# A graph layer on one core: mixer and gate groups of two tiles laid between expert tiles, norms in place, sums in freed columns

## What is computed

```python
xn = layernorm(x)
agg = segment_sum(xn[src] * edge_weight[:, None], dst)           # 106250 gathered rows
x2 = x + agg @ gnn_weight + mix(xn)                              # mix: linear attention over all rows
y = layernorm(x2)
top, idx = top_k(y @ gate_w + gate_b, 2); w = softmax(top)        # 16 experts, two for each row
moe = sum_k w[k] * (relu(y @ w1[idx[k]] + b1[idx[k]]) @ w2[idx[k]] + b2[idx[k]])
out = x2 + layernorm(y + moe) * gamma + beta
```

## Time and profile before

| | us |
|---|---|
| median of 3 runs | 1696.25 |
| lowest, highest | 1687.12, 1700.92 |
| the profiled execution | 1693.13 |
| its span (first to last instruction) | 1691.4 |
| outside the span | 1.7 |

### The profile page before, as it was taken

How to read it: one execution, slowest core, us unless ns; L and a number is a source line. 1 busy time by engine, 2 the same in 40 slices (tenths; PEclk the granted TensorE clock), 3 DMA queues, 4 the chain that set the end, 5 groups by cost and what they waited for, 6 DMA issues and landing times. The chain is left out here.

```text
span 1691.4 us, 25276 instructions
## 1 busy us (share of the span) xinstructions
PE 1204.5 (71%) x7570; PEld 944.3 (56%) x7570; DVE 586.8 (35%) x1778; ACT 490.3 (29%) x1323; POOL 1005.6 (59%) x1090
## 2 busy tenths in 40 slices
PE   0299989887605899885589887898968764356670
PEld 0155545556503788673378776777757653345560
DVE  6345445444500322332032231233213344344334
ACT  4033334332201333331133232233323232122221
POOL 3577777776377777677777767767763133231203
PEclk9999999999756999998699989898989887588885
DMA  9486333334245689787568968868994575545762
GB/s 336 138 277 205 106 104 106 105 104 117 63 163 184 181 275 321 239 293 239 193 183 308 324 241 315 305 223 301 398 309 162 212 270 168 202 149 206 256 240 84
DMA packets 173617, 363.98 MB, mean 215 GB/s; under 512 B 27968, under 2 KB 109248, under 8 KB 173344
## 3 DMA queue, kind: packets, MB, share of 16 engines
q1 hardware_dynamic: 80896, 186.89, 30.7%
q0 software_dynamic: 49296, 134.68, 25.6%
q10 hardware_dynamic: 43280, 40.65, 7.2%
HBM read 302.20 MB, written 59.90 MB: 214 GB/s over the span
## 5 line engine op out<-in xcount | busy, mean ns | idle before, releaser
L625 POOL DMA_INDIRECT ring<-normed_rows,src_sb x831 | 797.6, 960 | 331.9 <-issue 288.4
L1252 PE MATMUL ps<-room 128*128 128x128 f32 x2368 | 330.8, 300 | 56.2 <-DMA room<-in_w1b 42.3
L1252 PEld LDWEIGHTS ps<-room 128*128 128x128 f32 x2368 | 313.6, 214 | 66.5 <-issue 54.0
L1265 PE MATMUL ps<-room 128*128 128x256 f32 x1184 | 294.9, 394 | 16.3 <-issue 10.6
L1063 DVE TENSOR_TENSOR aggT<-ps,room 128x256 f32<-128x256 f32 x173 | 73.1, 423 | 612.4 <-PE ps L1265 572.7
L616 POOL DMA_INDIRECT ring<-results_by_slot,slot_i x98 | 97.5, 995 | 266.9 <-DMA results_by_slot<-aggT 125.4
L1265 PEld LDWEIGHTS ps<-room 128*128 128x128 f32 x1184 | 224.7, 200 | 45.1 <-issue 19.1
L739 ACT ACTIVATE room<-ps,room 128x128 f32<-128x128 f32 x592 | 168.8, 368 | 217.4 <-PE ps L1252 213.5
L1128 PE MATMUL ps<-ring,S 128*32 128x256 f32 x1680 | 119.9, 424 | 133.1 <-issue 102.2
L1155 PE MATMUL ps<-room,tT 128*128 128x512 f32 x392 | 181.6, 607 | 0.1
L1128 PEld LDWEIGHTS ps<-ring,S 128*32 128x32 f32 x1680 | 53.6, 118 | 170.9 <-issue 132.8
(11 more groups left out here) (148 smaller groups left out, 1143.8 us busy)
## 6 DMA issues: line engine op xcount, KB each, us to landing
room<-in_w2b SPq DMA_DIRECT2D x119, 640.0 KB, 5.7
room<-in_w1b SPq DMA_DIRECT2D x119, 514.0 KB, 6.4
room<-rows_by_slot SPq DMA_DIRECT2D x173, 128.0 KB
results_by_slot<-aggT ACTq DMA_DIRECT2D x173, 128.0 KB
ring<-normed_rows,src_sb POOLq DMA_INDIRECT x831
normed_rows<-X SPq DMA_DIRECT2D x7, 896.0 KB, 8.1
X<-in_x ACTq DMA_DIRECT2D x49, 128.0 KB, 2.4
result<-ring SPq DMA_DIRECT2D x49, 128.0 KB, 1.9
```

Of the source, the lines that this page charges most:

```text
L625: pool.indirect_dma_start(out=ring[:, b % 2 * BT + m, :], out_offset=None, in_=table, in_offset=bass.IndirectOffsetOnAxis(ap=src_sb[:, b * ...
L1252: mm = pe.matmul(hps[:, f * TS:(f + 1) * TS], w1_sb[g % WB][:, k * F + f * P:k * F + (f + 1) * P], xgT[s][:, k, :], start=(k == 0), stop=( ...
L1265: mm = pe.matmul(ops, hT[s][:, f, :], w2_sb[g % WB][:, f * D:(f + 1) * D], start=(f == 0), stop=(f == FC - 1))
```

## The change

1. Groups of mixer and gate have two tiles (`MG` 5 to 2): 26 groups where there were 12.
2. `plan()` is new. It keeps an estimated time of PE and of the gathers and fills each slot until PE would be 3 us past the next batch's landing. `emit` gives one mixer, gate, rank or slots; after each comes one expert tile. The projections use the same rule, so three stand in more of the slots.
3. `scatter` is queued three slots after `slots`, not two.
4. The gate normalizes rows in place in `X2`; gate and scatter read them there and `tile_in` is gone. Since `x2` is lost by that, the mixer first writes `x2 + beta` to the `aggT` columns of its tile, which nobody needs any more (`last`, one DVE add for each tile; ACT waits for it, `w_done`).
5. `fin1` no longer has ACT write normalized rows, since `X2` holds them: DVE adds the first result straight to them. `fin2` has no add of beta.
6. There are three buffers for `fin` groups, not two. A pick waits for the store of the group three before.
7. In the tail, `fin2` of a group and `fin1` of the next stand together, then three expert tiles. SP's `store` is late by one group: at `fin2` of a group it writes the one before.
8. The routing scratch moves out of `aggT` into its own buffer; one semaphore counts all scatters.

```diff
-MG = 5
+MG = 2
+FB = 3
@@ plan(): the estimates
-KV_SLOTS = 20
-ROOM = 12.8
-EXPERT = 4.5
+GATHER, EDGES_PE, KV_PE, MID_PE, MIX_PE, GATE_PE, TAKEN_PE, LEFT_PE = 1.254, 2.1, 5.0, 11.0, 2.1, 1.0, 3.75, 1.5
+LAG = 3.0
@@ plan(): emit and expert
+    def emit(work, b, part_ready):
+        if routes:
+            what, p = routes.pop(0)
+            work.append((what, p))
+            if what == "slots":
+                ready[p] = b + 4
+                pool[min(b + 3, NB)].append(("scatter", p))
+                tiles.extend((p, j) for j in range(NPOS[p]))
+            return 0.5
+        if len(gates) > 1 or gates and not (mixes and complete(GROUPS[mixes[0]][1] - 1) <= b):
...
+            return GATE_PE * (GROUPS[g][1] - GROUPS[g][0])
+        if mixes and complete(GROUPS[mixes[0]][1] - 1) <= b:
...
+            return MIX_PE * (GROUPS[g][1] - GROUPS[g][0])
+        return 0.0
@@ plan(): the loop over batches
+        now = max(now, landed) + EDGES_PE
+        until = landed + GATHER * (BT + sum(2 * (PT[w[1] + 1] - PT[w[1]]) for w in pool[b])) + LAG
+        while now < until:
...
+            now += emit(slots[b], b, ready)
+            now += expert(slots[b], b)
@@ plan(): the tail
+    def next_fin():
+        if begun_fins:
+            tail.append(("fin2", begun_fins.pop()))
+        if todo and (PART[FIN[todo[0]][0]] < (tiles[0][0] if tiles else NPART)):
+            begun_fins.append(todo[0])
+            tail.append(("fin1", todo.pop(0)))
     while tiles:
+        next_fin()
         for _ in range(3):
+            expert(tail, NB + 4)
@@ SP
+            late = []
+            def fin2(f):
+                for o in late:
+                    store(o)
+                late[:] = [f]
@@ POOL, pick
-                if prior is not None:
-                    pool.wait_ge(f_summed, FIN_AT[FIN[prior][1] - 1] + 1)
+                after(pool, f_out[i], 16 * fin_before(f))
@@ ACT, gate; fin1 of ACT is removed
-                    after(act, scattered[i], 32 * sent_before(PART[q], i))
-                    act.activation(tile_in[:, i, :], X2[:, q, :], ACT.Identity, bias=nmr[:, q:q + 1],
+                    act.wait_ge(w_done, GATE_AT[q] + 1)
+                    act.activation(X2[:, q, :], X2[:, q, :], ACT.Identity, bias=nmr[:, q:q + 1],
@@ DVE, mix
+                def last(q):
+                    dve.tensor_tensor(last_add[q], X2[:, q, :].rearrange("p (k n) -> p k n", k=KD),
+                                      beta_b[:, :].rearrange("p (k n) -> p k n", k=KD), ALU.add).then_inc(w_done, 1)
...
                 agg.then_inc(y_stats, 1)
+                for q in range(a, b):
+                    last(q)
@@ DVE, fin1
+                    dve.scalar_tensor_tensor(out=z, in0=z, scalar=prob[:, 0, q:q + 1], in1=X2[:, q, :],
+                                             op0=ALU.mult, op1=ALU.add).then_inc(f_half, 1)
@@ DVE, fin2
-                    dve.tensor_tensor(X2[:, q, :], X2[:, q, :], beta_b[:, :], ALU.add).then_inc(f_scaled, 1)
...
-                    dve.scalar_tensor_tensor(out=z, in0=z, scalar=f_r[:, n:n + 1], in1=X2[:, q, :],
+                    dve.scalar_tensor_tensor(out=z, in0=z, scalar=f_r[:, n:n + 1], in1=last_add[q],
```

More of the change, by code:

```diff
@@ L92, in plan @@
     pool = [[] for _ in range(NB + 1)]
[L93 to L121, removed]
@@ L122, in plan @@
-    tail = slots[NB]
[L124 to L140, removed]
@@ new lines, in expert @@
+    def expert(work, b):
+        if not tiles or ready[tiles[0][0]] > b:
+            return 0.0
+        p, j = tiles.pop(0)
+        work.append(("moe", p, j))
+        return TAKEN_PE if j < SURE[p] + 9 else LEFT_PE
+    for b in range(NB):
+        landed += GATHER * BT
+        now = max(now, landed) + EDGES_PE
+        until = landed + GATHER * (BT + sum(2 * (PT[w[1] + 1] - PT[w[1]]) for w in pool[b])) + LAG
+        while now < until:
+            before = now
+            if kvs:
+                slots[b].append(("kv", kvs.pop(0)))
+                now += KV_PE
+                if not kvs:
+                    slots[b + 1].append(("mid", 0))
+                continue
+            if ("mid", 0) in slots[b + 1]:
+                break
+            if slots[b] == [("mid", 0)]:
+                now += MID_PE
+            now += emit(slots[b], b, ready)
+            now += expert(slots[b], b)
+            if now == before:
+                break
+        landed += GATHER * sum(2 * (PT[w[1] + 1] - PT[w[1]]) for w in pool[b])
@@ L142, in plan @@
+    tail = slots[NB]
+    while mixes or gates or routes:
+        emit(tail, NB - 1 if False else NB, ready)
+        if len(tiles) and ready[tiles[0][0]] < NB + 3:
+            expert(tail, NB + 3)
+    def next_fin():
[4 more added lines that the diff above has]
+            tail.append(("fin1", todo.pop(0)))
     while tiles:
+        next_fin()
@@ L154, in plan @@
+    while todo or begun_fins:
+        next_fin()
+    picks = [("pick", w[1]) for w in tail if w[0] == "fin1"]
+    pool[NB] = [w for w in pool[NB] if w[1] < NPART - 1] + picks[:2] + [("scatter", NPART - 1)] + picks[2:]
     return slots, pool
@@ L185, in fin_buffer @@
 def fin_buffer(f):
-    return FINS.index(f) % 2
+    return FINS.index(f) % FB
 def fin_before(f):
[L192 to L198, removed]
+    return sum(FIN[g][1] - FIN[g][0] for g in FINS[:FINS.index(f)] if fin_buffer(g) == fin_buffer(f))
 def positions_with(s, p):
@@ L599, in scatter @@
                         pool.wait_ge(xg_in[s], 16 * rows_loaded(s, p - 2))
[L600 removed]
+                for q in range(PT[p], PT[p + 1]):
                     for k in range(2):
@@ L746, in moe @@
                     store_y(p, j)
-            def fin1(f):
-                i = fin_buffer(f)
-                after(act, f_out[i], 16 * fin_before(f)[0])
-                for n, q in enumerate(range(*FIN[f])):
-                    act.activation(zt[i][:, n, :], X2[:, q, :], ACT.Identity, bias=nmr[:, q:q + 1],
-                                   scale=rstd[:, q:q + 1]).then_inc(z_row, 1)
             def fin2(f):
@@ L764, in _ @@
                     act.copy(accs[b % 2][:, :], acc[b % 2]).then_inc(acc_copied, 1)
-                run({"kv": kv, "mid": mid, "mix": mix, "gate": gate, "rank": rank, "moe": moe, "fin1": fin1,
-                     "fin2": fin2}, b)
+                run({"kv": kv, "mid": mid, "mix": mix, "gate": gate, "rank": rank, "moe": moe, "fin2": fin2}, b)
         @block.vector
@@ L1213, in turn_y @@
                     pe.wait_ge(y_normed, GATE_AT[q] + 1)
-                    turn("gate", q, tile_in[:, q - PT[PART[q]], :])
+                    turn("gate", q, X2[:, q, :])
                 turn_y(a)
```

85 lines of the change are left out of this document (47 added, 38 removed).

## The result

| | median of the runs | range | runs |
|---|---|---|---|
| before | 1697.78 us | 1687.12 to 1704.14 | 20 |
| changed | 1689.93 us | 1676.31 to 1698.35 | 20 |

The ratio is 0.995, with a 95% interval from 0.993 to 0.9971: half a per cent faster, where 1.6% was forecast. The direction was right, and the time lies inside the range, but the gain is under a third of the one forecast. The profiled execution of the changed kernel has a span of 1689.8 us, beside 1691.4 before.

The account below looks back on a forecast made before the run. PE's own work was the largest term, busy 71% of the span. Batch 27 at 547, plus 830 to batch 69 and 288 of tail, ended at 1665 against 1691.4 profiled; 1670 us on the median's scale, range 1625 to 1725.

Parts of the forecast that it names:

- The tail: From batch 69 to the end: 288 us against 402, with full cycles of 17 us instead of 23.7.
- the picks don't bind: Tail cycle: with three buffers the picks are ready in time, so 13.7 us is the floor.
- SP's earlier release: Tail cycle: SP's store is of the group before, so it no longer waits and loads rows and weights earlier.
- The projection packed in front: Before batch 27: two projections, about 10 us, go into PE's waits for gathers; `mid` ends near 374, or 384.
- Part 0, 10.6 a pair: Before batch 27: seven mixer and gate pairs without expert tiles between, 74 us; batch 27 at 547, bound 557.
- Behind batch 27, 9.5 a pair: Batches 27 to 69: a pair costs 4.8 + 2.3 + 2.4 us, a single 6.6; 22 us more than before.
- my second rival: Gates: the second load of x is usually late, stalling each of 17 gates 3.2 us more; 1724 us, chance 18%.
- The sign I had set: Waits for the second load of x above 4 us in the mean would show the forecast wrong to the slow side.
- my case: Whole kernel: the forecast of 1670 us with its own range, 1645 to 1695, given 52%.
- Scatter1: Behind batch 42: 30.7 us of scatter and 15.1 of gather lie bare, 46 us; 17 more than before.
- ten expert tiles at 4.4: Batches 27 to 69: ten more expert tiles than before, taken out of the tail, add 44 us.
- Later scatters: Batches 27 to 69: scatter1 adds 17 us, scatter2 7, scatter3 nothing; 24 in the sum.

Follow-up runs that it names:

- on_time: Changed kernel with SP's stores of a finished group in their own place, not a group later; ratio 1.0186 on a slow chip.
- groups5: Changed kernel with mixers and gates of up to five tiles instead of two, its planner kept; 1642.18 us, ratio 0.967 on a good chip.
- old_ahead_room: Old order, new tail, second load of x three tiles ahead, plus 14.5 instead of 12.8 units of work a slot; 0.9842 on a slow chip.

## Why the forecast missed

The changed kernel's span against the terms of the sum, by the profiled executions:

| term | forecast | measured |
|---|---|---|
| to batch 27 | 547 | 558.6 |
| batch 27 to 69 | 830 | 840.4; 807.1 without the second load of x |
| tail | 288 | 290.8 |
| end | 1665 | 1689.8 |

- *The tail*: right in size, and in mechanism but for one step. Ten `fin` cycles from 1455.2 to 1626.1 take 170.9 us (169.5 forecast), 17.1 each, where the old cycle took 23.7. But they run from 12.4 to 19.9, and "the picks don't bind" was wrong: in five of the ten VectorE waits for fetched results, 17.0 us together, and GpSimd's picks wait 76.9 us (8 times) for stores, which are late by design. So the close match of the mean is in part luck. I had put the short cycle down partly to SP's earlier release; on_time speaks against this part of the reason, on a slow chip.
- *The projection packed in front*: right. Batch 20 stands at 384.3, `mid` and the first two mixers behind it included, and 10 us were won there.
- *Part 0, 10.6 a pair*: this step failed. A pair takes 12.2 to 13.9 us (without the edges between). The wait in it was 3.0, as forecast within half a microsecond. What was left out is that the clock is low behind it each time: the mixer of a pair takes 5.9 to 7.5 us there, and the sum had 4.8. I charged the clock in the tail, where rows of before show it, and not here, where only groups of five stood in the rows. The mean of four pairs is 13.0, 2.4 more than in the sum; the copy after batch 23 stands at 472.0, 11 later than forecast, and batch 27 12 later, past the 557 that I had called the bound.
- *Behind batch 27, 9.5 a pair*: this step failed by the second load of x, 33 us for the 15 pairs and singles between batches 27 and 69, 2.2 us each, of which 1.5 are TensorE's longer wait for the gate's row. That is my second rival, for which I had put the turning point at 1.5 us a gate. Against it I held the mean wait of 1.8 us in the earlier trace rows, but that mean came from groups of five, in which one wait is shared by five tiles. The sign I had set, over 4 us in the mean, is met only if the wait at the scatter is counted (193.0 / 47 = 4.1). It was too high: with 3.2 the load already cost this much. I also made it an alternative to my case, with a chance, where it was a term with a size.
- *The rest of that stage* was priced 23 us too dear (807.1 against 830), which hides two thirds of those 33. Scatter1 was right: 45.9 us from batch 42 to 43, 46 forecast. That leaves the later scatters, ten expert tiles at 4.4 and the pairs at 9.5; the runs don't tell these apart.
- *Later scatters*: forecast at 24 us against the old place, 15 found by undoing it.
- *What hiding tiles is worth*: the deeper error of the prediction was not to price this. With the new tail an expert tile costs the tail (316.8 - 290.8) / 7 = 3.7 us between the old order and the new (52 and 45 positions behind batch 69, so seven of the ten tiles come out of the tail and three out of the time before batch 27; the tail of groups5 gives 3.6), not the 23.7 / 3 = 7.9 of the old cycle. In the loop it costs TensorE at least the same 3.73. So the new order moves work between two places where it costs about the same, and pays for it with small groups and a later scatter. old_ahead_room, on a slow chip, shows a move that costs more than it gives: eight tiles moved cost the loop 82 us and gave the tail 40.

The losses of the new order, from 1614 to 1690: groups 48 (with what they have in common with the 29 of the second load of x), scatter 15, and 13 not assigned. They were found one at a time and need not add up exactly.

The fastest kernel of the study is the old order with the new tail and storage: 1613.74 us, 0.949.

## What to carry to other kernels

Price a moved piece of work at both places as they will be after the change: once the tail's cycle was short, hiding more of it was worth no more than it cost in the loop. When a group is cut smaller, look in the rows for what stands behind every pause at its ends, and charge the pause as idle and the matmuls behind it at the clock they are granted. And a rival that can be true in part belongs into the sum as a term with its size.

## What the runs showed of the hardware that was not expected

The same kernel took 1613.74 us on one chip and 2163.42 on another. Its waits on TensorE there, the slow chip first, then the good one:

```profile
PE ps L1254 <- issue: 260.3, 46, 16.0
PE ps L1130 <- issue: 83.5, 44, 44.3
```

```profile
PE ps L1130 <- issue: 89.9, 13, 46.5
...
PE ps L1254 <- DMA room<-in_w1b: 24.9, 25, 2.4
```

Over all its lines TensorE idles 505 us in 182 pieces with nothing recorded that it waits for, against 117 us in 31. It happens within straight runs of matmuls too, here the edges of one batch on the slow chip, where the good one takes 1.50 us for all 24:

```profile
255.99 1.48 PE L1130 MATMUL ps<-ring,S 128*32 128x256 f32 x18
258.29 0.38 PE L1130 MATMUL ps<-ring,S 128*32 128x256 f32 x1 [0.82 <-issue]
258.99 0.41 PE L1130 MATMUL ps<-ring,S 128*32 128x256 f32 x2 [0.32 <-issue]
259.72 0.38 PE L1130 MATMUL ps<-ring,S 128*32 128x256 f32 x1 [0.32 <-issue]
260.43 1.03 PE L1130 MATMUL ps<-ring,S 128*32 128x256 f32 x2 [0.34 <-issue]
```

GpSimd's gathers are as quick as elsewhere (959 and 965 ns), and so are the transfers with a recorded landing (a chunk of the first load of x: 11.6 and 11.3 us). No run tested where this idle time comes from, and the cause stays open. What it means for a study is shown: on slow chips leaving out x stood at 1.008 and 1.012, behind the earlier scatter in the same series (1.006 and 1.007), where on good chips it stands ahead of it (0.979 against 0.985), and the old order with the new tail stood at 0.975 instead of 0.949. The large effects kept their order there, the small ones did not, and no mechanism can be sized by such a ratio.
